# Attention recurrence: VectorE's order of one slot rewritten, key scaling last, GpSimd's fades and the key stores moved

## The reference, cut to what matters

```python
q = l2norm((x @ Wq).reshape(Bb, Tt, H, K)) / np.sqrt(K)   # 16 heads of 16
k = l2norm((x @ Wk).reshape(Bb, Tt, H, K))
v = v * beta;  k_beta = k * beta;  g = cumsum(decay)      # chunks of 64 rows
P = where(strict, einsum(k_beta, k) * L, 0)               # L = exp(g_i - g_j)
Ainv = (I + P)(I + P^2)(I + P^4)...                       # 64 x 64 per head and chunk
v = Ainv @ v;  k_cumdecay = Ainv @ (k_beta * exp(g))
def step(S, inp):                                         # over the chunks
    v_new = v_i - kcd_i @ S
    o_i = q_i * exp(g_i) @ S + attn @ v_new
    S_new = S * exp(g_last) + einsum(k_i * exp(g_last - g_i), v_new)
o = o * rsqrt(mean(o * o) + 1e-5) * norm_w * silu(gate);  x = x + o @ Wo
```

## Time and profile before

| | us |
|---|---|
| runs shown, three | 4384.79, 3293.92, 1240.54 |
| their median | 3293.92 |
| the profiled execution | 1235.57 |
| its span, first to last instruction | 1233.8 |
| busy in the span: PE / DVE / ACT / POOL | 1038.0 / 925.7 / 599.7 / 405.8 |
| attention slots n = 7 to 31, 308.01 to 729.64 | 421.6 |

### The profile page before, as it was taken

One profiled execution on the slowest core, in us unless ns is written; L12 is line 12 of the kernel. 1 busy time (PEld: TensorE's weight loads), 2 busy tenths in 40 slices (PEclk: granted clock), 3 DMA queues, 4 the chain that ended last, 5 costly groups with the idle time before them and its releaser, 6 DMA issues. The chain is left out here.

```text
span 1233.8 us, 38552 instructions
## 1 busy us (share of the span) xinstructions
PE 1038.0 (84%) x15542; PEld 739.6 (60%) x15542; DVE 925.7 (75%) x2403; ACT 599.7 (49%) x1614; POOL 405.8 (33%) x580
## 2 busy tenths in 40 slices
PE   2999977778888888788898886679999798799878
PEld 2888853445555565555565565458888574355455
DVE  3777736358999999999988988528776345899853
ACT  2433336434767676777766765554332452101052
POOL 2666630311222121222121211216665257400055
PEclk9999988886999999999989987779999798899979
DMA  9000013244444444444434443100000034954013
GB/s 251 20 2 1 1 27 141 69 87 98 104 101 103 94 97 86 102 106 104 100 78 99 102 94 71 42 2 1 1 1 1 18 74 104 232 160 115 1 35 103
DMA packets 282625, 93.31 MB, mean 76 GB/s; under 512 B 208976, under 2 KB 275408, under 8 KB 282448
## 3 DMA queue, kind: packets, MB, share of 16 engines
q1 hardware_dynamic: 247056, 84.03, 28.3%
q10 hardware_dynamic: 35392, 6.82, 2.9%
HBM read 56.20 MB, written 30.41 MB: 70 GB/s over the span
## 5 line engine op out<-in xcount | busy, mean ns | idle before, releaser
L1777 DVE TENSOR_TENSOR delta_tmp<-delta_PR 128x130 f32<-128x130 f32 (+12 forms) x416 | 152.9, 368 | 9.4
L1774 DVE TENSOR_TENSOR delta_PR<-delta_PR,delta_tmp 128x130 f32<-128x130 f32 (+12 forms) x416 | 152.1, 366 | 9.3
L1889 POOL TENSOR_TENSOR delta_S<-delta_E,delta_Bm 128x128 f32<-128x128 f32 x32 | 15.3, 477 | 282.2 <-issue 273.3
L1427 PE MATMUL psum<-delta_T,delta_pad 128*32 128x128 f32 x2048 | 81.2, 325 | 31.9 <-DMA delta_T<-inverse_scratch 31.4
L1626 ACT ACTIVATE delta_y<-psum 32x128 f32<-32x128 f32 x256 | 68.7, 268 | 80.1 <-PE psum L1461 58.2
L1427 PEld LDWEIGHTS psum<-delta_T,delta_pad 128*32 128x32 f32 x2048 | 69.6, 131 | 41.7 <-DMA delta_T<-inverse_scratch 38.2
L507 POOL TENSOR_TENSOR ffn_H<-ffn_hid,ffn_H 128x512 fp32r<-128x512 f32 x48 | 61.8, 1292 | 57.5 <-DVE ffn_H L473 57.5
L1642 ACT ACTIVATE delta_wide<-delta_S 32x128 f32<-32x128 f32 x256 | 78.2, 306 | 3.2
L507 POOL TENSOR_TENSOR first_H<-first_hid,first_H 128x512 fp32r<-128x512 f32 x48 | 61.7, 1292 | 53.9 <-DVE first_H L473 53.9
L1411 PE MATMUL psum<-delta_MV,delta_KT 32*32 32x128 f32 x2048 | 68.9, 287 | 10.6 <-ACT delta_E L1576 10.6
L1865 POOL TENSOR_TENSOR delta_VK<-delta_QK,both_eg 128x256 f32<-128x256 f32 x32 | 20.8, 650 | 156.6 <-DVE delta_QK L1709 156.5
(11 more groups left out here) (282 smaller groups left out, 2594.8 us busy)
## 6 DMA issues: line engine op xcount, KB each, us to landing
within_scratch<-delta_PT SPq DMA_DIRECT2D x128, 64.0 KB, 1.9
delta_PR<-within_scratch SPq DMA_DIRECT2D x16, 512.0 KB, 4.3
inverse_scratch<-delta_PR SPq DMA_DIRECT2D x16, 512.0 KB, 3.0
space_T<-taps_scratch SPq DMA_DIRECT2D x8, 1024.0 KB, 5.9
X<-taps_scratch SPq DMA_DIRECT2D x8, 1024.0 KB, 8.9
X<-in_x SPq DMA_DIRECT2D x32, 128.0 KB, 10.2
turned_scratch<-gates_XT SPq DMA_DIRECT2D x16, 256.0 KB, 2.3
delta_xT<-turned_scratch SPq DMA_DIRECT2D x32, 128.0 KB, 3.8
```

The source lines that it names most:

```text
L1427: i = pe.matmul(bank[3][SUB * c:SUB * c + SUB, (2 * w + g) * P:(2 * w + g + 1) * P], M.pad[:, from_c:from_c + SUB], M.T[t % 2][:, h * P:(h ...
L1774: i = v.tensor_tensor(after, after, t3, ALU.add)
L1777: i = v.tensor_tensor(t3, column.to_broadcast([P, j, n_after]), row.to_broadcast([P, j, n_after]), ALU.mult)
```

## The change

On VectorE the order of one slot is new. `add_o` and `new_stats` move from the slot's end to the next slot's begin, behind the first `own_heads` and `new_state`, with `faded_q` and `sum_qk` behind them; the solve steps then run in longer stretches; `scale_qk`, formerly behind step 9, comes after all 29, and `keep_within`, `keep_attn` and `scale_o` follow it. A last `add_o(NT - 1)` stands behind the loop. On GpSimd `middle_state` waits for `s_x` (the first `new_state`) instead of `s_bm` (the first `own_heads`), and `fade_first` for the next tile is issued at the end of the slot. On SyncE the key stores and key loads are issued one slot later.

```diff
@@ delta_sync
         at(decays_in, n)
-        at(keys_out, n - 1)
-        at(keys_in, n - 2)
+        at(keys_out, n - 2)
+        at(keys_in, n - 3)
@@ delta_vector
         at(own_heads, Z, 0)
-        solve(n, 0, 1)
         at(new_state, Z, 0)
-        solve(n, 1, 3)
+        at(add_o, O - 1)
+        at(faded_q, n - LAG_FORM)
         at(sum_qk, n)
-        solve(n, 3, 6)
-        at(faded_q, n - LAG_FORM)
-        solve(n, 6, 10)
+        if O - 1 < AHEAD * BLK:
+            at(new_stats, O - 1)
+        solve(n, 0, 9)
+        at(own_heads, Z, 1)
+        solve(n, 9, 10)
+        at(new_state, Z, 1)
+        solve(n, 10, 15)
+        at(keep_gate, n)
+        solve(n, 15, 25)
+        at(sum_o, Z)
+        solve(n, 25, 29)
         at(scale_qk, n)
-        solve(n, 10, 11)
-        at(own_heads, Z, 1)
-        solve(n, 11, 12)
-        at(new_state, Z, 1)
-        solve(n, 12, 15)
-        at(keep_gate, n)
-        solve(n, 15, 21)
-        at(sum_o, Z)
-        solve(n, 21, 24)
         at(keep_within, n - LAG_FORM)
-        solve(n, 24, 25)
         at(keep_attn, n - LAG_FORM)
-        solve(n, 25, 29)
         at(scale_o, Z)
-        at(add_o, O)
-        if O < AHEAD * BLK:
-            at(new_stats, O)
+    add_o(NT - 1)
@@ delta_gpsimd
     def middle_state(t):
         g.wait_ge(S.s_e, 2 * t + 1)
-        g.wait_ge(S.s_bm, 2 * t + 1)
+        g.wait_ge(S.s_x, 2 * t + 1)
@@
-        at(fade_first, Z)
         at(middle_state, Z)
         at(fade_second, Z)
         at(gate_o, n - LAG_OUT)
         at(decayed_k, n)
         at(kept_k, n)
+        at(fade_first, Z + 1)
```

## The result

The changed kernel takes 1304.0 us (median; 1301.7 to 1310.2), 1.054 times the kernel before [1.046, 1.061]; its profiled span is 1304.4 us against 1233.8.

A forecast was written before the change was run, and what follows sets the result against it. VectorE, 93% busy, was taken to bound the slots. Slots 7 to 31 +29 us, 4 to 6 +5.7, 1 to 3 +1.5, the last -2: total +34, 1270 us; range 1250 to 1288, for 8 in 10 1238 to 1298.

The forecast's parts named there:

- Gain: VectorE's slots: stretching beside GpSimd's work goes entirely, 1.4 us per slot, some 35 us before any wait.
- full blocks: VectorE beside GpSimd: were every GpSimd job a full block, up to 3.8 us per slot freed, some 95 us.
- the two forecast terms: VectorE's slots: 1.4 us per slot gained from stretching, 0.7 us per slot lost to fewer breaks in the solve.
- The chain from `scale_qk`: Slot's begin: project_qk waits for scale_qk, so own_heads comes 2.5 and faded_q 4.7 us after it; VectorE idles 2.2 us.
- The T tiles of the odd slots: Odd slots: TensorE does not make them later, needing 4.7 us from outputs to from_state's end; 17.5 or 18.05 us each.
- Even slots, a queue: SyncE's pair_back behind the late keep_within leaves at 2.7 us, second own_heads at 8.8; even slots take 18.3 us.
- One ring instead of several: Slots 7 to 31: slot length summed along the wait from scale_qk through project_qk and keep_kq to faded_q, +29 us.
- Slots 4 to 6: Solve without scan: 16.3 us each, 48.9 against 43.2, +5.7 us; slots 1 to 3 ahead of them, +1.5.
- The last slots: Slots 32 to 35, without scale_qk: keep only the gain but wait for the recurrence, -2 us of at most -5.
- The clock: Rival: TensorE's clock falls while idle before project_qk, 2.95 us become 4.7 in 12 slots, +21, 1291 us; chance 0.20.
- What costs nothing: middle_state behind new_state, fade_first at the slot's end, later add_o and key stores: no cost; one store wait, 3 us once.
- the forecast case: The chain in every slot of the recurrence, 1270 us; chance 0.50.

The follow-up runs named there:

- scale_only: Kernel before, with scale_qk alone moved from behind step 9 to behind step 28: 1274.9 us, ratio 1.031.
- keeps_only: Kernel before, with keep_within and keep_attn alone moved from steps 24 and 25 to behind step 28: 1289.2 us, ratio 1.043.
- faded_sync: Changed kernel with faded_q behind step 5 and, on SyncE, pair_back and inverse_in ahead of within_out: 1258.6 us, ratio 1.017.
- faded_back: Changed kernel with faded_q alone moved back behind step 5: 1290.8 us, ratio 1.043.
- sync_order: Changed kernel with SyncE's list reordered: pair_back ahead of within_out in odd slots, inverse_in ahead of within_out and pair_in in even ones: 1294.8 us, ratio 1.046.
- scale_keeps_back: Changed kernel with scale_qk behind step 9 and keep_within, keep_attn around steps 24 and 25 again: 1315.4 us, ratio 1.063.
- back_sync: Changed kernel with scale_qk behind step 9 again and, on SyncE, pair_back and inverse_in ahead of within_out: 1303.4 us, ratio 1.054.
- adds_behind_gate: Changed kernel with faded_q behind step 5, scale_qk behind step 9, sum_o behind step 20, SyncE's list reordered, add_o and new_stats behind keep_gate: 1342.9 us, ratio 1.086.
- first_part: Kernel before, with only new_state, add_o, new_stats, sum_qk ahead of step 0, and GpSimd's wait and the stores as changed: 1244.6 us, ratio 1.006.
- ring_stats: Changed kernel with faded_q behind step 5, scale_qk behind step 9, sum_o behind step 20, SyncE's list reordered, new_stats behind keep_gate: 1267.4 us, ratio 1.025.
- short_ring: Kernel before; to_state, turn_kq ahead of project_qk, keep_kq ahead of squares, sum_qk behind step 8, scale_qk behind 15, second own_heads and new_state one step later: 1263.1 us.

## Why the prediction was wrong

- **Gain**: near. The durations of VectorE's instructions in the 25 slots add up to 411 us for 441, 30 us less for the 35 forecast (95 with full blocks). With the lost overlaps its busy time falls by 15 us (390.5 to 375.7), for the 17.5 of the two forecast terms.
- **The chain from `scale_qk`**: right to 0.1 us in 17 of the 25 slots (`faded_q` 4.68 or 4.69 us behind it, for 4.7), and the odd slots from 9 to 19 take 18.07 to 18.2 us, but for 13, for the 18.05 forecast. In the other eight it is 5.8 to 6.6 us long. `scale_only` shows this cause: +38 us alone. That it was the only one was wrong.
- **The T tiles of the odd slots** are the step that failed. For these slots I wrote that TensorE does not make them later, and put the term at nothing. There `within_out`, the wait for its landing, `pair_in` and SyncE's T loads follow each other behind the late keeps, and I had not followed that queue to `apply` and to the next `project_qk`. The runs show `apply` waiting for T in odd slots (1.8 to 4.2 us in 11 of the 13) and the next `project_qk` late behind the longest of these waits; four of the eight long chains begin the even slot behind such a slot (13, 21, 23, 25). The four issues themselves are no longer than before (1.92 to 3.58 us, mean 2.3; before 1.93 to 3.30, mean 2.2): it is their place that changed. `keeps_only` prices the late keeps at 51 us alone, `faded_sync` against `faded_back` SyncE's order at 32 us within the change, `sync_order` at 9.
- **"Even slots, a queue"**: followed rightly and sized too small. `pair_back` leaves 2.66 us behind the end of `scale_qk` at the soonest, for 2.7, but at 3.15 on average; ScalarE's T loads are issued at 6.5 for 6.0, and the second `own_heads` starts at 9.6 for 8.8. With the long chains the even slots are 0.9 us longer than forecast, 10.7 of the 19.5 us missing in the 25 slots; the odd ones are the other 8.8.
- **One ring instead of several**: the forecast added up one way round, through `scale_qk`. `faded_q`'s new place had no price of its own; `scale_keeps_back` and `back_sync` show that the slot stays as long with `scale_qk` back in its old place.
- **Slots 4 to 6**: +5.7 forecast, +11.6 measured: they take 54.8 us for 43.2 in the windows; what lies ahead of them takes 3.9 more, for 1.5. `project_qk` takes 3.75 us there for 1.98, at half clock, behind a wait of 6.60 us for `scale_qk`:

```profile
299.89 3.75 PE L1371 MATMUL psum<-both_w_in,delta_xT 128*128 128x512 f32 x4 [6.60 <-DVE delta_QK L1709]
```

- **The last slots**: -2 forecast, +6.8 measured. Slots 32 and 33 take 17.9 us each for 15.5 and 14.2, at a clock of 0.71 for 0.78 and 0.76. Runs with SyncE's new list have 503 to 507 us behind slot 31 (`adds_behind_gate` apart, 523) and those with late keeps and the old list 508 to 511, which fits the T tiles; no run was made for it alone.
- **The clock** was a rival at 0.20, in twelve places ahead of `project_qk`. The trace has 65 us at the low level in the slots instead of 24, in fifteen places: eight beside a wait of `apply` for T (38 us), four beside one of `to_state` for `keep_y` (17 us), two beside one of `project_qk`, one beside one for `keep_gate`. So the clock fell, but hardly where the rival had it, and on top of the forecast case, where the two were priced as alternatives.
- **What costs nothing**: the moved fades and GpSimd's wait show no wait of VectorE for GpSimd in the 25 slots, and no wait for the key stores is in TensorE's list either. `add_o`'s move to the slot's begin was taken as free too. `first_part`, with `add_o`, `new_stats` and `sum_qk` there, is not faster than before; which of its moves takes the gain back was not separated.

## What to carry to other kernels

In a pipeline of slots with lists in order on every engine, moving an operation costs by the rings that it closes, through all engines and DMA queues back to itself, one slot later. Write down each ring's length before the change and after it: several can be nearly equal, and then undoing one part shows little. Here two parts that cost 38 and 51 us alone are in a change that costs 68, and the same edit of SyncE's list is worth 9 us or 32 depending on the others. Saving 1.2 us of stretching per slot (30 us in 25 slots) was paid for with 2.6 us of waits. Making one operation early is no rule either, since it then stands ahead of another: `keep_gate` early in odd slots won 33 us, `scale_qk` early won 10 us with SyncE's old list and lost 9 with the new one.

## What the runs showed of the hardware

The same 9715 matrix products took 359.6 us in one order of the lists and 379.0 in another, with a granted clock of 0.96 and 0.91. Slots 7 to 31 had the clock at half speed for 17 to 140 us over all runs, against 24 in the kernel before. The longest came with long waits for `keep_gate` (99 us in `back_sync`, 109 in `ring_stats`) and for `turn_o`'s bank (140). Not every wait does it: in the changed kernel waits of 3.1 and 3.3 us in slots 8 and 9 passed at full clock, where one of 2.8 us in slot 13 did not, and `short_ring`, with slots of 447 us, has 17 us in all. With an unneeded product ahead of the wait for `scale_qk`, that time was 44 us for 65, in one traced execution each.

The stretching of VectorE beside GpSimd depends on the operands, as the first rows say: two inputs in SBUF, 559 ns; the same steps away from GpSimd's work, 247. `own_heads`, which reads PSUM, took 282 and 289; in the kernel before 25 of its 50 ran beside a GpSimd job, at 280 ns, as did the other 25. `scale_o` (L1808), beside GpSimd's last jobs in the changed kernel, went from 418 to 461 ns.
